# SyncE's 2 KB name loads at the head of each step of a graph network's edge stage

## The reference

```python
edge_index = jnp.stack([src, dst])
h = jnp.maximum(_layernorm(x, axis=-1), 0.0)
x = x + _L0_gnn_ref(h, L0_gnn_W_l, L0_gnn_W_r, edge_index)   # mean over the edges' h[src] at dst; @ W_l.T, + h @ W_r.T
h = jnp.maximum(_layernorm(x, axis=-1), 0.0)
x = x + _L1_gnn_ref(h, edge_index, edge_attr_128, W1, b1, g1, be1, W2, b2, g2, be2, W3, b3)
# L1: agg = segment_sum(edge_attr, src, N); h = concat([x, agg]); h = bn(silu(h@W1+b1)); h = bn(silu(h@W2+b2)); h@W3+b3
```

## Time and profile before

| | us |
|---|---|
| median of 3 runs | 1403.31 (1402.49 to 1404.88) |
| the profiled execution's own time | 1399.47 |
| its span | 1397.7 |
| B, from the first scatter into `acc2` to the last | 407.8 |

### The profile page before, as it was taken

How to read it: one execution, slowest core, us unless ns; L and a number is a source line. 1 busy time by engine, 2 the same in 40 slices (tenths; PEclk the granted TensorE clock), 3 DMA queues, 4 the chain that set the end, 5 groups by cost and what they waited for, 6 DMA issues and landing times.

```text
span 1397.7 us, 22052 instructions
## 1 busy us (share of the span) xinstructions
PE 1015.3 (73%) x5275; PEld 736.5 (53%) x5275; DVE 1074.9 (77%) x4647; ACT 876.5 (63%) x1708; POOL 879.4 (63%) x625
## 2 busy tenths in 40 slices
PE   0227677777666666665999898898887667999776
PEld 0225555555544445553666566665655554447765
DVE  2428888888877667666999989898974887788966
ACT  1227676776766556553887777686775776669610
POOL 7778888888888888876777777777771000002443
PEclk9969999999999878888999999899997778999999
DMA  9988888877766666667899989998988994216999
GB/s 330 370 303 209 219 217 204 222 160 169 173 154 136 136 155 135 141 139 188 218 245 237 246 216 236 231 234 220 234 202 289 358 353 160 90 60 233 418 418 370
DMA packets 184860, 315.35 MB, mean 226 GB/s; under 512 B 21904, under 2 KB 73526, under 8 KB 184770
## 3 DMA queue, kind: packets, MB, share of 16 engines
q1 hardware_dynamic: 116602, 266.54, 54.4%
q0 software_dynamic: 62720, 38.57, 23.0%
q10 hardware_dynamic: 5448, 9.29, 1.8%
HBM read 163.49 MB, written 150.84 MB: 225 GB/s over the span
## 4 chain that ended last, share of the span: by engine, by line
POOL 42%; DMA 24%; issue 17%; PE 10%; DVE 5%; ACT 1%; SPq 1%; DVEq 0%; POOLq 0%; ACTq 0%
POOL acc L906 21%; POOL acc L926 9%; DMA acc<-zT,target_b 8%; POOL xin L884 7%; DMA acc<-tabs,target_b 6%; PE ps L1770 6%; DMA zT<-x_dram 4%; POOL zT L892 4%; DMA zT<-z_dram 2%; DMA xin<-acc 2%; PE ps L1780 1%; PE ps L1740 1%; DVE zT L1588 1%; DMA acc<-zT,tabs 1%; DVE zT L1592 1%
## 5 line engine op out<-in xcount | busy, mean ns | idle before, releaser
L906 POOL DMA_INDIRECT acc<-zT,tabs x196 | 316.4, 1614 | 67.2 <-issue 62.0
L1636 PE MATMUL ps<-zT 128*128 128x512 f32 (+5 forms) x784 | 260.8, 481 | 133.4 <-ACT zT L1045 127.0
L1636 PEld LDWEIGHTS ps<-zT 128*128 128x128 f32 (+1 forms) x784 | 158.7, 208 | 258.2 <-issue 129.7
L1371 DVE BATCH_NORM_STATS2 zT<-zT 128x6 f32<-128x128 f32 (+1 forms) x384 | 78.9, 278 | 166.5 <-DMA zT<-in_x_dram 166.5
L926 POOL DMA_INDIRECT acc<-zT,target_b x100 | 156.5, 1565 | 53.8 <-issue 25.8
L926 POOL DMA_INDIRECT acc<-tabs,target_b x96 | 150.3, 1565 | 49.3 <-issue 23.7
L884 POOL DMA_INDIRECT xin<-in_x_dram,tabs x140 | 143.2, 1023 | 42.6 <-issue 42.1
L1005 ACT ACTIVATE hT<-ps 128x1024 f32<-128x1024 f32 (+1 forms) x100 | 100.1, 1003 | 61.4 <-PE ps L1628 47.8
L1669 PE MATMUL ps<-wr,hT 128*128 128x128 f32 (+1 forms) x784 | 105.5, 292 | 35.5 <-DVE zT L1362 35.5
L1669 PEld LDWEIGHTS ps<-wr,hT 128*128 128x128 f32 (+1 forms) x784 | 101.7, 206 | 42.6 <-issue 40.1
L1628 PE MATMUL ps<-ident,zT 128*128 128x128 f32 (+1 forms) x784 | 117.5, 299 | 8.4 <-ACT zT L997 8.0
(11 more groups left out here) (199 smaller groups left out, 2280.7 us busy)
## 6 DMA issues: line engine op xcount, KB each, us to landing
acc<-bst SPq DMA_DIRECT2D x12, 2112.0 KB, 19.9
acc<-bst SPq DMA_DIRECT2D x48, 528.0 KB
zT<-in_x_dram SPq DMA_DIRECT2D x48, 512.0 KB, 6.4
zT<-acc SPq DMA_DIRECT2D x48, 512.0 KB, 4.6
zT<-x_dram SPq DMA_DIRECT2D x42, 512.0 KB, 9.9
out_dram<-zT SPq DMA_DIRECT2D x42, 512.0 KB, 10.2
zT<-row_dram SPq DMA_DIRECT2D x49, 256.0 KB, 5.6
zT<-in_edge_attr_dram SPq DMA_DIRECT2D x48, 256.0 KB
```

The source lines that it names most:

```text
L906: pool.indirect_dma_start(acc1, bass.IndirectOffsetOnAxis(ap=target_a[:, k, j:j + 1], axis=0), v[:, j, :], None, compute_op=ALU.add).then_ ...
L1636: ins = nc.tensor.matmul(psA[:, 0:j + 1, 0:p], t[0:p, j, :], same[0:p, par, at:at + j + 1, 0:p], start=(j == ROWS - 1), stop=(j == 0))
```

## The change

`load_b_edges` no longer loads the halves. A function of its own, `load_b_halves`, does so, and each step of SP calls it right behind the step's first wait, for one round further on: step r now loads the halves of round r + 5, and the wait for the spreading of round r + 3's names stands there as well. Before, that step's end loaded round r + 4's and waited for the spreading of round r + 2's. The first step loads two rounds' halves, four and five. The edges' rows stay where they were, with their own waits.

```diff
@@ -648,15 +648,18 @@
+            def load_b_halves(i, par):
+
+                if i:
+                    sp.wait_ge(*spread(par, i - 1))
+                sp.dma_start(halves[:, par, :], src_halves[2 * i + par]).then_inc(B["row_loaded"][par], 16)
+
             def load_b_edges(i, par, tail, spill, held=False):
 
                 r = 2 * i + par
                 p = EDGE_TAIL if tail else P
-                if type(i) is not int or i:
-                    sp.wait_ge(*spread(par, i - 1))
                 if held:
                     sp.wait_ge(*two_ago(s_end2, par, i - 1, 16))
-                sp.dma_start(halves[:, par, :], src_halves[r]).then_inc(B["row_loaded"][par], 16)
                 sp.wait_ge(*two_ago(B["summed"], par, i))
...
@@ -667,18 +670,23 @@
                 sp.wait_ge(*this(s_sc2, par, i, 32))
-                if not before and ahead:
+                if not before:
+                    load_b_halves(2, 0)
                     load_b_nodes(*ahead)
+                if 2 * i + par + 5 <= RF:
+                    load_b_halves(*divmod(2 * i + par + 5, 2))
                 if third and third[3]:
```

More of the change, by code:

```diff
@@ L669, in _ @@
                 sp.wait_ge(*this(s_sc1, par, IT - 2, 64))
+                load_b_halves(0, par)
                 load_b_edges(0, par, False, 0)
@@ L673, in _ @@
             for par in range(2):
+                load_b_halves(1, par)
                 load_b_edges(1, par, False, 0)
```

## The result

| | kernel before | changed kernel |
|---|---|---|
| median us (lowest to highest, runs) | 1403.75 (1396.45 to 1409.79, 6) | 1420.86 (1418.58 to 1422.58, 6) |
| profiled execution us (its span) | 1399.47 (1397.7) | 1419.42 (1417.7) |
| stage B, first to last start of a scatter into the second sums | 644.1 to 1052.05 = 408.0 | 644.48 to 1068.87 = 424.4 |
| behind B, to the span's end | 345.6 | 348.8 |

The changed kernel is slower: 1.0127 times the kernel before, interval 1.0103 to 1.015. Two executions, one of the kernel before (1981 us) and one of e13 (3308 us), were far slower than all others and count in no ratio. Of the 20.0 us between the two profiled executions 0.4 lie ahead of B, 16.4 in B and 3.2 behind it; the medians are only 17.1 us apart, mainly since the profiled execution of the kernel before lies 4.3 us under its median. What follows is on B.

The account below looks back on a forecast made before the run. B's pace was taken to be set by POOL's loop of scatter issued, landed, next scatter, not by PE. Four terms of 0 us each left the median at 1403.3, predicted as 1403 us, range 1394 to 1410.

Parts of the forecast that it names:

- PE's wait on the halves goes.: In B, nearly all of PE's 34.5 us and most of DVE's 26.1 go; 0 us on the path, bound -51.7.
- The halves' issue moves.: In SP's queue, edges' rows go out 0.3 us earlier; bounds +-11.8 us over 38 landing waits, taken as 0.
- The doubt about the slow issue: In SP's queue: if a full queue causes the slow issue, not the halves, the edges' rows would take long.
- SP now waits for PE.: SP's new wait at B's start makes loads late, covered by about 5 us of slack: 0 us, otherwise 13 us.
- Hardly any after step 6: SP's waits on PE's matmul: about 5 us in steps 1 and 2, hardly any after step 6.
- The two ends.: Before the first scatter the same load order, at the end the last scatter and x1 as before: 0 us.
- C: Rival: SP's new wait makes DVE wait for nodes; slower by 4 to 13 us, 1407 to 1416; chance 0.06.
- D: Rival: PE still stands at line 1681 for halves, time unchanged at 1403; 0.41 together with the forecast.
- C's sign: What would show rival C: DVE waits for `acc`, the nodes, at line 1454.
- A: Rival: POOL's landings get shorter; faster, 1397 at half the 11.8 us bound, 1391.5 at the full; chance 0.36.
- B: Rival: ACT's earlier z store meets the second scatter; slower, 16 rounds by 0.5 us, 8 us, 1411; chance 0.17.
- The argument against it: Against the rival of z meeting the scatter: a z that is over earlier also frees the next round; no size given.

Follow-up runs that it names:

- e13: Changed kernel, but halves of round r + 4 at step's head, z held until its round's first two scatters landed, unread 2 KB load before edges' rows: 1407.89 us, 1.002.
- e4: Changed kernel with an eighth of each full round's z stored in B, part of the computation left out: 1405.05 us, 0.9997 of the kernel before.
- e5: Kernel before with an eighth of each full round's z stored, part of the computation left out: 1396.57 us, 0.9956 of the uncut kernel before.
- e11: Kernel before with each z store held until its round's fourth scatter has landed, near the next round's second scatter: 1418.18 us, 1.0075.
- e7: Changed kernel with halves of round r + 4 at the step's head and an unread 2 KB load between nodes and edges' rows: 1418.55 us, 1.0105.
- e2: Changed kernel with halves of round r + 4, not r + 5, at the step's head, so SP never stands there for PE: 1420.34 us, 1.0119.
- e3: Changed kernel with each z store held by ACT until the first two scatters of its round have landed: 1418.58 us, 1.0085.
- e10: Changed kernel with halves of round r + 4 at the step's head and an eighth of z stored, part of the computation left out: 1406.56 us, 1.0000.

## Why the prediction was wrong

The forecast was 1403.0, no change; it is slower by 1.27%, outside the range.

1. *PE's wait on the halves goes.* The first half was right: 34.5 us became 1.6, DVE's for the names' matmul 26.1 became 14.8 (I had said under 10). The step that failed is its conclusion, "On the path: 0 us", with the bound only on the side of a gain. That POOL has 8.6 us of slack to the data says that earlier data wins nothing; it doesn't say that it loses nothing, because ACT's z store goes with that work and comes into the landings that POOL waits for. What the runs show in place of the 0: B 16.4 us longer, all of it in POOL's landing waits; of the 1.27% z's bytes at their new place carry about two thirds (e4 and e10 against e5; e11 shows the effect in the kernel before). The lead was also mis-sized: "up to about 3 us further ahead" was 4.3 in the mean, because PE came to rest only at the edges' rows, which it now waits 41.7 us for.

2. *The halves' issue moves.* Its sign was undecided and its bounds were +-11.8 us. Behind the nodes the edges' rows moved 0.6 us earlier in the mean instead of 0.3, since the halves' issue and the gap ahead of it both went (1.1 us to 0.5). Against the second scatter they moved 0.7 to 1.5 us. The doubt about the slow issue was right: it is the edges' rows' that now takes long (0.76 us for 0.37). e7 puts the spacing back and wins nothing that its interval shows.

3. *SP now waits for PE.* At the start it went as computed. SP's timeline of steps 1 and 2 of the changed kernel answers to the earlier trace rows:

```profile
667.07 0.26 SPq L655 DMA_DIRECT2D zT<-half_dram  x1
667.42 0.38 SPq L580 DMA_DIRECT2D x_dram<-xin  x1
667.89 0.42 SPq L573 DMA_DIRECT2D zT<-acc  x1
...
673.85 0.26 SPq L655 DMA_DIRECT2D zT<-half_dram  x1
674.20 0.38 SPq L573 DMA_DIRECT2D xin<-y_dram  x1
...
675.23 0.38 SPq L573 DMA_DIRECT2D zT<-acc  x1
```

Nodes at 667.89 (I had 668.9), y at 674.20 (674.9), nodes at 675.23 (676); DVE took the nodes of rounds 4 and 5 at 677.74 and 685.20, 0.7 and 1.0 us earlier than before. "Hardly any after step 6" was wrong:

```profile
SPq L654 <- PE ps L1689: 45.2, 26, 9.2
```

22 of these waits and 23.9 us of them lie in 690 to 1040. PE runs ahead, stops for the edges' rows of a round and spreads the next names only behind them. e2, without them, is no faster within its +-0.5%.

4. *The two ends.* Ahead of B 0.4 us, behind it 3.2 in one profile of each: not settled.

The rivals: C and D are out (e2; the wait did go). C's sign did show, DVE waits 36.0 us for nodes where it waited 3.6, but e2 has it too (34.2 us) without SP's wait: DVE waits because it is ahead, and POOL doesn't wait for its data, so the sign couldn't tell C. A had the wrong sign. B was the mechanism, with the right place: z's store, second scatter, 16 rounds. It had 0.17, and its price was too low: 0.5 us a round as a guess against 1.66 us in 12 rounds, less 0.13 us in the other 29. z came 3.4 us earlier in the mean instead of up to 2.5. "It decides once z falls within about 1 us of the edges' rows" tied it to a neighbour that doesn't decide: in e7 the edges' rows are back in these rounds and the loss isn't gone. The argument against it, that an early z frees the next round, is worth at most the 3.8 us won in the other 29 rounds, against 19.9 lost.

The Trainium skill's rule that I set aside, of "DMA: Bandwidth & Descriptors", section "Queues, rings and completion order", says that a completion waits for that DMA engine's earlier writes on its other queues. I turned it down on one pair of edges' rows. The runs agree with its direction for z: a store on ACT's queue, in flight with a scatter of POOL's queue, puts that landing, and with it the next round, off by 1.1 us (e11, 6.51 us for 5.46) to 1.7 us (changed kernel, 8.27 for 6.61). That it is the order of the writes, and not the shared bandwidth, no run here shows; where z was issued 0.1 us behind the scatter (e11) it was not the earlier one by issue.

## What to carry to other kernels

An engine with slack isn't free to run earlier: its DMA issues run with it, so before you speed it up, list what it and the engines that follow it issue, and see where these land against the transfer that sets the pace. Where a loop is paced by a landing, give the slack row two prices, one for a gain and one for a loss. If a large store of another engine may drift, tie its issue to that landing (here the hold cost nothing in the kernel before, 1.0002, and took 1.0119 to 1.0023; with SP's wait for PE in place it gave back only a third, e3).

## What the runs showed of the hardware that was not expected

- A 512 KB store issued from 1.1 us before to 1.8 us behind an indirect scatter-add put off the next round by 1.7 us in the mean (8.27 us against 6.61 in the same 12 rounds without it there), and by 1.2 us within e11 (7.88 against 6.68). With 64 KB in its place the rounds with z took 6.94 and 6.95 us (e4, e10; 6.62 in the kernel before).
- It goes both ways: the store's own median time to landing rose from 4.5 to 6.5 us.
- The long DMA issue goes with the place in SP's sequence, not with the load. The issue of the halves behind the nodes took 0.46 us in the mean, that of the edges' rows behind them 0.37; with the halves moved, theirs took 0.27 and that of the edges' rows, now directly behind the nodes, 0.76. With a small load back between them (e7) it was 0.37 again, and that small load's issue took 0.59.
